# A two-layer gated cross-attention kernel: second attention's maxima through ScalarE and GpSimd, its first scores inside the first expert stage, its second half of queries placed by TensorE

## The reference

```python
x = x + tanh(g_xattn[0]) * attention0(layernorm(x), ctx)  # 16 heads of 64, causal mask
x = x + tanh(g_ffn[0])   * experts0(layernorm(x))         # 8 experts + 4 identity ones, top 2
x = x + tanh(g_xattn[1]) * attention1(layernorm(x), ctx)  # 16 heads of 8, no mask, biases
x = x + tanh(g_ffn[1])   * experts1(layernorm(x))         # 8 routed (top 2) + 2 shared experts
# attention1, per sequence and head:
attn = softmax(q @ k.T / sqrt(8)); out = (attn @ v) @ Wo.T + bo
```

## Time and profile before

| | |
|---|---|
| median of 3 runs | 275.26 us (273.01, 275.26, 275.41) |
| the profiled execution | 273.14 us, span 271.1 us from the first to the last instruction |
| busy: PE, DVE, ACT, POOL | 247.6, 190.0, 110.5, 69.6 us |
| first attention | to about 123 us |
| first expert stage | 123 to 184.4 us |
| second attention | 184.4 to about 231 us |
| second expert stage | to 267 us, then the store |
| mean granted TensorE clock | 0.996 of 2.4 GHz |

### The profile page before, as it was taken

How to read it: one execution, slowest core, us unless ns; L and a number is a source line. 1 busy time by engine, 2 the same in 40 slices (tenths; PEclk the granted TensorE clock), 3 DMA queues, 4 the chain that set the end, 5 groups by cost and what they waited for, 6 DMA issues and landing times.

```text
span 271.1 us, 7236 instructions
## 1 busy us (share of the span) xinstructions
PE 247.6 (91%) x2956; PEld 210.0 (77%) x2956; DVE 190.0 (70%) x478; ACT 110.5 (41%) x187; POOL 69.6 (26%) x83
## 2 busy tenths in 40 slices
PE   8879989899999999989999998998798988879992
PEld 3558878788998888769999997997576877757881
DVE  1537798967365989896256586438788998879753
ACT  2565545544441554323134453430636454221220
POOL 2355393445433533340010031001122001111000
PEclk9999999999999999999999999999999999999998
DMA  6519600030000000598499100340052000000011
GB/s 200 188 45 321 175 1 4 2 157 4 0 2 2 1 2 7 87 147 308 189 169 171 49 0 0 118 116 1 2 174 63 2 2 5 0 0 4 8 30 41
DMA packets 14705, 18.98 MB, mean 70 GB/s; under 512 B 2384, under 2 KB 11472, under 8 KB 14544
## 3 DMA queue, kind: packets, MB, share of 16 engines
q1 hardware_dynamic: 14528, 18.26, 25.6%
q10 hardware_dynamic: 144, 0.26, 0.5%
HBM read 13.80 MB, written 4.72 MB: 68 GB/s over the span
## 4 chain that ended last, share of the span: by engine, by line
PE 66%; DVE 16%; issue 5%; DMA 4%; ACT 4%; POOL 2%; SPq 1%; DVEq 0%
PE OC L1130 9%; PE MB L1090 5%; PE MB L980 5%; PE SP L1051 5%; PE OC L1073 5%; PE TP L1060 4%; PE MB L982 4%; PE MB L981 4%; PE TP L1243 3%; PE MB L1202 2%; PE MB L1206 2%; PE OC L1079 2%; DMA w_raw<-in_w 2%; PE SP L982 2%; PE SP L980 2%
## 5 line engine op out<-in xcount | busy, mean ns | idle before, releaser
L398 POOL TENSOR_TENSOR S_sb<-S_sb,nmax 128x512 f32<-128x512 f32 x32 | 33.2, 1039 | 38.9 <-DVE nmax L701 38.9
L798 DVE SCALAR_TENSOR_TENSOR x_sb<-OC,gate,x_sb 128x128 f32<-128x128 f32 x64 | 18.0, 345 | 26.8 <-PE OC L1130 26.8
L1130 PEld LDWEIGHTS OC<-f_w,hid 128*128 128x128 f32 x256 | 30.9, 192 | 1.4
L692 DVE TENSOR_TENSOR S_sb<-SP,maskb 128x512 f32<-128x512 f32 x32 | 21.9, 686 | 13.5 <-PE SP L1051 13.3
L1130 PE MATMUL OC<-f_w,hid 128*128 128x128 f32 x256 | 31.0, 275 | 0.0
L701 DVE TENSOR_REDUCE nmax<-S_sb 128x4 f32<-128x512 f32 x32 | 22.0, 686 | 1.1
L507 ACT ACTIVATE PT<-TP 128x512 f32<-128x512 f32 x32 | 19.0, 593 | 7.8 <-PE TP L1060 7.7
L1060 PE MATMUL TP<-id_sb,S_sb 128*128 128x128 f32 x128 | 19.6, 275 | 2.4 <-POOL S_sb L398 2.4
L368 POOL TENSOR_SCALAR var_eps<-mv 128x4 f32<-128x4 f32 x8 | 2.0, 245 | 70.9 <-DVE mv L646 70.9
L1073 PE MATMUL OC<-PT,arena_f 128*32 128x128 f32 x512 | 17.6, 275 | 2.3 <-issue 1.7
L1060 PEld LDWEIGHTS TP<-id_sb,S_sb 128*128 128x128 f32 x128 | 14.9, 141 | 5.6 <-POOL S_sb L398 3.9
(11 more groups left out here) (187 smaller groups left out, 582.5 us busy)
## 6 DMA issues: line engine op xcount, KB each, us to landing
arena_f<-in_zeros SPq DMA_DIRECT2D x1, 2048.0 KB, 14.5
w_raw<-in_w SPq DMA_DIRECT2D x4, 384.0 KB, 4.0
k_dram<-f_r SPq DMA_DIRECT2D x3, 512.0 KB, 13.9
arena_r<-k_dram SPq DMA_DIRECT2D x4, 384.0 KB
arena_r<-q_dram SPq DMA_DIRECT2D x16, 96.0 KB
ew_raw<-in_f0w SPq DMA_DIRECT2D x1, 1024.0 KB, 6.0
f_w<-in_f0w SPq DMA_DIRECT2D x1, 1024.0 KB, 9.8
row_dram<-f_r SPq DMA_DIRECT2D x2, 512.0 KB, 3.1
```

The costliest lines, as they stand in the source:

```text
L398: g.tensor_tensor(S_sb[:, b], S_sb[:, b], nmax[:, b].unsqueeze(2).to_broadcast([P, H4, P]), ALU.add).then_inc(shifted, 1)
L692: v.tensor_tensor(S_sb[:, b].rearrange("p (r a) k -> p r a k", r=2), SP[:, :, 2 * P * b:2 * P * (b + 1)].rearrange("p r (a k) -> p r a k", ...
L1130: ins = mm(OC[:, n % 2, batch(t)], hid[:, n % 2, c, batch(t)], f0_w2[:, e, c, :], start=(c == 0), stop=(c == 1))
```

## The change

It touches the second attention on all engines, the order of the first expert stage's second half, and the second expert stage's first steps.

- `shift1(b)` moves from VectorE to GpSimd. ScalarE first copies the transposed maxima to SBUF (`maxima1` on ScalarE, into `NMT`).
- The row sums of `outputs1` stand in 4 columns instead of being repeated over 128 (weights `row_of` in place of `col_sel_sb`). ScalarE copies values and sums to SBUF (`copy_outputs`), VectorE transposes the sums, takes the reciprocal of 16 numbers a partition and transposes back with a repeat; GpSimd multiplies (VectorE for the last sequence).
- Scores of sequence 0 and the first half of those of sequence 1 are computed inside the first expert stage (n = 13 to 15), in the ring banks (`SPARE`), with their maxima on VectorE at n = 12 and 13.
- Routing of the first expert stage's second half is one step sooner; `queries1(0)` is at n = 10 instead of 11.
- Keys and queries are placed by one DMA of all 128 partitions instead of four of 24 partitions; the DMAs that placed the rows of ones are gone. For the second half of the tokens there is no DMA at all: TensorE spreads the rows with 0/1 weights (`spread_queries`, 4 times 2 matmuls) and ScalarE copies them to `q1s` (`place_queries`).
- From sequence 3 on, `values_of(b - 2)` stands ahead of `maxima1(b)`, and `sums_of(b - 2)` behind the scores.
- The first half's output projection is one call; ScalarE scales it and GpSimd adds it to `x_sb` (`scale_output`, `residual1` on GpSimd).
- `keep_clock` runs: 24, 16, 16, 6 and 10 matmuls before, one of 12 now.
- VectorE in the last stage: `route_best(1, 0)` ahead of `normalise1(7)`, `route_gates(1, 0)` ahead of the loop; the second half's routing one step later.

```diff
+SPARE = [("s", 0, 0), ("s", 0, 1), ("t", 0, 0)]
+AREAS = [("s", 1, 0), ("s", 1, 1), ("t", 0, 1)]
@@ SyncE
-                for j in range(4):
-                    sp.dma_start(dst[32 * j:32 * j + 24, :, tok].bitcast(F32),
-                                 dram.rearrange("(j i) r t -> j r i t", j=4)[j]).then_inc(moved, 16)
+            def place_heads(dst, dram, moved):
+                sp.dma_start(dst.bitcast(F32), dram.rearrange("i p t -> p i t")).then_inc(moved, 16)
...
+            for w in range(2):
+                tok = slice(2 * P * w, 2 * P * (w + 1))
+                place_heads(q1s[:, :, tok], q_dram[:, :, tok], q_moved[w])
@@ GpSimd
+            def shift1(b):
+                pool.wait_ge(max_out, b + 1)
+                wait_queries(pool, b)
+                g.tensor_tensor(q1s[:, :, batch(b)], q1s[:, :, batch(b)].bitcast(F32),
+                                NMT[:].unsqueeze(1).to_broadcast([P, 4, P]), ALU.add).then_inc(shifted1, 1)
+            def residual1():
+                pool.wait_ge(scaled, 1)
+                g.tensor_tensor(x_sb[:, seqs(0), :], x_sb[:, seqs(0), :], xn[:, seqs(0), :], ALU.add).then_inc(res, 1)
+            def normalise1(b):
+                pool.wait_ge(o_sum1, 3 * (b + 1))
+                g.tensor_tensor(oT1[:, batch(b)], o_sb[:, b % 2, 0:P], R1[:, b % 2], ALU.mult).then_inc(o_done1, 1)
...
+            for b in range(2, B):
+                shift1(b)
+                if b == B - 2:
+                    residual1()
+                    continue
+                if b == B - 1:
+                    rstd_of(3, 0)
+                    normalise1(b - 3)
+                normalise1(b - 2)
                 for hook in hooks.get(b, ()):
                     hook()
@@ ScalarE
+            def maxima1(b):
+                name = ("m", b)
+                wait_full(act, name)
+                if b:
+                    act.wait_ge(shifted1, b)
+                sc.activation(NMT[:], ring(name)[:, 0:P], ACT.Copy).then_inc(max_out, 1)
...
+            for i in range(4):
+                place_queries(i)
+            hooks = {2: [lambda: split_f1(0), lambda: split_f1(1)], 3: [lambda: split_f1(2), lambda: split_f1(3)]}
+            for b in range(2, B):
                 for hook in hooks.get(b, ()):
                     hook()
+                if b > 2:
+                    copy_outputs(b - 2)
+                if b == B - 2:
+                    scale_output()
                 exp1(b, 0)
+                if b + 1 < B:
+                    maxima1(b + 1)
                 exp1(b, 1)
+            copy_outputs(B - 2)
             xnT_hi_copy(3, 0)
+            copy_outputs(B - 1)
@@ VectorE
             def normalise1(b):
...
+                dve.wait_ge(o_copied, b + 1)
+                v.transpose(sumT[:], o_sb[:, b % 2, P:2 * P].rearrange("p (c r) -> p c r", r=32)).then_inc(o_sum1, 1)
+                dve.wait_ge(o_sum1, 3 * b + 1)
+                v.reciprocal(rsum1[:], sumT[:, :, 0:4]).then_inc(o_sum1, 1)
...
+            xnT_lo_copy(3, 0)
             normalise1(B - 2)
-            xnT_lo_copy(3, 0)
+            route_best(1, 0)
             normalise1(B - 1)
-            route_best(1, 0)
...
+            route_gates(1, 0)
+            hooks = {0: [residual1, lambda: gates_lo(0), lambda: stats_after(3, 1)], 1: [lambda: normed(3, 1)],
```

More of the change, by code:

```diff
@@ L413, in _ @@
             pool.wait_ge(consts, 4)
-            for b in range(2):
+            for b in range(4):
                 const(row_of[:, b, b:b + 1], 1.0)
@@ new lines, in _ @@
+            xnT_lo_copy(2, 1)
+            max1(2, 0)
+            queries1(1)
+            max1(2, 1)
+            for b in range(2, B):
+                if b == B - 1:
+                    normalise1(b - 3)
+                    normed(3, 0)
+                    normalise1(b - 2)
+                    break
+                max1(b + 1, 0)
+                max1(b + 1, 1)
+                if b == B - 2:
+                    stats_after(3, 0)
+                else:
+                    normalise1(b - 2)
@@ L991, in fill_wait @@
                 name = ("w", b)
-                done(name, keep_clock(take(name)[:, 0:256], 16 if b < 2 else 6))
+                done(name, keep_clock(take(name)[:, 0:256], 12))
             def xn_transposes(n, h):
@@ L1189, in maxima1, with values_of @@
                 bank = take(name)
-                if b == 0:
-                    keep_clock(bank[:, 256:512], 24)
                 pe.wait_ge(maxed1, 2 * (b + 1))
                 done(name, nc.tensor.transpose(bank[:, 0:P], NM[:], id_sb[:]))
-            def outputs1(b):
+            def values_of(b):
                 bank = take(("o", b))
@@ L1205, in outputs1, with output1 @@
                         rows = slice(32 * j, 32 * (j + 1))
-                        ins = mm(bank[rows, P:2 * P], col_sel_sb[:, i, rows], PT1[b % 3][:, j, i, :],
+                        ins = mm(ring(name)[rows, P:2 * P], row_of[:, i, :], PT1[b % 3][:, j, i, :],
                                  start=(i == 0), stop=(i == 3))
-                done(("o", b), ins)
-            def output1(h, w):
-                name = ("y1", h, w)
+                done(name, ins)
+            def outputs1(b):
+                values_of(b)
+                sums_of(b)
+            def output1(h):
+                name = ("y1", h)
                 bank = take(name)
-                pe.wait_ge(o_done1, HB * h + 2 * w + 2)
-                for b in range(2):
-                    ins = mm(bank[:, batch(b)], oT1[:, batch(HB * h + 2 * w + b)], wo1_sb[:], start=True, stop=True)
+                pe.wait_ge(o_done1, HB * (h + 1))
+                for b in range(HB):
+                    ins = mm(bank[:, batch(b)], oT1[:, batch(HB * h + b)], wo1_sb[:], start=True, stop=True)
                 done(name, ins)
@@ L1358, in _ @@
                 if n == 2:
+                    xn_transposes(3, 1)
+                if n == 3:
                     logits(1, 1)
```

392 lines of the change are left out of this document (215 added, 177 removed).

## The result

| | median of 20 runs | lowest | profiled execution (span, mean granted clock) |
|---|---|---|---|
| before | 274.08 us | 272.15 | 273.14 us (271.1, 0.996) |
| changed | 276.16 us | 273.19 | 273.26 us (271.4, 0.985) |

The account below looks back on a forecast made before the run. TensorE and VectorE were taken to bound the attention's period together. 2.3 us gained less 0.7 lost made 1.6, so 273.14 became 271.5 us profiled, 273.7 from the median; forecast 272.5, range 267.5 to 277.

Parts of the forecast that it names:

- Step 1: First expert stage: 1.1 us gained from a wait, 1.0 us new wait at scores1(0, 0), last experts end at 186.5 us.
- Step 2: Opening of the second attention: transposed scores of sequence 3 start at 205.9 us, 2.0 us gained.
- Step 3: Steady sequences of the second attention: period 3.55 instead of 4.25 us, three exceptions, logits at 229.2, 2.3 us gained so far.
- Step 4: Last stage, logits to last expert group: 35.3 instead of 34.6 us, TensorE standing 2.8 us; 0.7 us lost.
- rival 3: TensorE's clock falls in the last stage's 2.8 us wait: 2.5 us lost, net 0.9 slower, 274.0 us; chance 0.12.
- My sum without a clock: Whole kernel: 2.3 us gained less 0.7 lost, 1.6 us gained, the profiled 273.14 becoming 271.5 us.
- rival 1: Queries land in time (1.0), and late shift 4 (1.9) or output1(0) wait (1.1) is absent: 4.5 us gained, 268.6; chance 0.28.
- Rival 2: GpSimd's shift decides every attention sequence: gain gone at 1.55 us a shift, 2.7 us lost at 2.0; chance 0.15.
- port rule: Last stage, GpSimd's product of sequence 6 beside the router: one engine held an estimated 0.4 us, making the gain 1.2 us.

Follow-up runs that it names:

- both_filled: Changed kernel with early exponential table and warm matmuls in the attention's opening, ahead of output1(1) and ahead of the second expert1: ratio to the kernel before 0.9952.
- exp_table: Changed kernel with one 128x1 exponential behind maxima1(0), so that its table is loaded early: ratio to the kernel before 1.0117.
- shift_vector: both_filled with the shifts of sequences 2 to 7 back on VectorE, reading ScalarE's copy of the maxima: ratio to the kernel before 0.9994.
- tail_fill: Changed kernel with 20 warm matmuls ahead of the wait of output1(1) and 16 ahead of the second expert1: ratio to the kernel before 0.9964.
- after_nofill: Changed kernel with its last warm matmuls cut from 12 to 1: ratio to the kernel before 1.0045, or 1.0147 by the medians of all runs.
- order_turn2: Changed kernel with VectorE's last-stage order rewritten, early exponential table, 26 warm matmuls in fill_wait(0), 5 each ahead of turned1(1,0) and turned1(2,0): ratio to before 0.9894.
- all_filled: tail_fill and exp_table together, with 26 warm matmuls in fill_wait(0) and 6 ahead of each turned1(b,0) from sequence 1 on: ratio to the kernel before 0.9999.
- opening_filled: Changed kernel with early exponential table, 26 warm matmuls in fill_wait(0), 5 each ahead of turned1(1,0) and turned1(2,0): ratio to the kernel before 1.0107.
- order_fill: Changed kernel with VectorE's last-stage order rewritten, early exponential table and 26 warm matmuls in fill_wait(0): ratio to the kernel before 0.9894.
- before_nofill: Kernel before without its warm matmuls of the second attention and last stage (two runs left out, three cut to one each): ratio to the kernel before 0.9998.
- stats_first: Changed kernel with VectorE's statistics of sequences 4 to 7 ahead of gates_lo(0): ratio to the kernel before 0.9933, or 1.0008 by the medians of all runs.

## Why the prediction was wrong

The step that failed is the last one of the sum, in two terms. It put nothing for TensorE's clock, which I had as a rival at 0.12 and at one place: the changed kernel was below full clock in all its 20 runs (0.942 to 0.985), and lost 0.2 us for each 0.001. And it put the last stage at 0.7 us lost: 1.9 were lost at full clock and 3.6 in the profiled run. At full clock 1.0 us of my 1.6 was there (both_filled); the clock took it and more.

**Step 1, the first expert stage: right, its wait too long.** The 1.19 us wait is gone (163.67, no idle). No wait of 1.0 us came at `scores1(0, 0)`: it ran at 176.19 behind `hidden0(14)`. The low part was done at 168.2 (168.7) and the placement issued 3.6 us later, the lower of the two values I had (3.6 and 5.3), and landed 4.0 us from its issue: taking the middle made the wait. Last experts end at 185.5, 1.0 us sooner than forecast.

**Step 2, the opening: right to 0.6 us, in part by luck.** Transposed 3 at 205.34 (forecast 205.9), though 19.9 us behind the last experts rather than 19.35: the microsecond won in step 1 hides half a one lost here. Of my chain one link was missing: the exponential's table, 1.28 us, is loaded only when its first input is there, at 186.24. exp_table shows that it cost next to nothing.

**Step 3, the steady sequences: right.** L417 takes 1.273 us (1.28). Sequence 4 waits 1.13 us for its shift behind the splits, period 4.83 (5.45); sequence 5 3.98 (3.55); `output1(0)` waits 0.94 (1.1); logits at 228.83 (229.2). What VectorE was relieved of by the shift did not matter at full clock, though: shift_vector.

**Step 4, the last stage: this failed.** "0.7 us lost" was 3.6. TensorE's wait of 2.8 us was 2.73, but I had second experts at 12.75 us and they came at 13.35; I counted the statistics ahead of the product, and not that TensorE would stand 2.27 us. At full clock the stage is 36.5 us (tail_fill), 1.2 over my 35.3; the clock adds 1.65. Of the 1.2, 0.35 is a slip of mine: second experts 0.35 later and 0.7 at n = 6 make 35.65, not 35.3. Another 0.55 is the second experts, and 0.3 lies in the steps up to n = 5; n = 6 cost 0.8, as put.

**The clock** was rival 3, with a price of 2.5 us, one place and a chance of 0.12. Its sign came, a clock under 1.0 between 225 and 250 us; that a fallen clock turns the gain into a loss was right, and the chance far too low. The 4 us of matmuls in its price had no row; a dip of 3.4 us costs this stage 1.6. I put it behind the 2.8 us wait only. It fell behind the shorter wait after it (in the profiled run), and in the attention, where I had looked for none because TensorE has no wait over 1.3 us there.

Most of the medians' loss will lie in the attention: the profiled run, with its dip in the last stage, is at 0.985 and 273.26 us; the median run, 2.9 us slower, is at 0.968. That its dips lie in the attention is not shown, for no trace of it was kept, but likely: in the traces of after_nofill and exp_table, at 0.962 and 0.959, 14 and 17 us of dips lie there and 7 and 3 in the last stage. What I had in hand and didn't weigh: the change takes out four of five runs of warm matmuls, shortens the other and makes TensorE the bound, so a stretch at 1.2 GHz that would have cost nothing before can cost now.

My sum without a clock, 271.5 us, stands against 271.6 of the profiled run without its 1.65, 271.05 us of tail_fill's one run at 1.000 and 271.8 of both_filled. That it comes so near is in part luck: the 1.2 us of order that I missed in the last stage are balanced by logits 0.4 us sooner than put and a store 0.6 us shorter, which I had not counted. Of rival 1 one term came, the queries' 1.0 us, of which half was lost again in the opening; the waits of 1.13 and 0.94 us stayed. Rival 2 didn't come: GpSimd's shift held 1.27 us in all eight.

On the port rule of the Trainium skill ("SBUF — State Buffer", "SBUF: two separate sides"): the product of sequence 6 ended at 230.16, before the router's first instruction with two SBUF inputs at 230.37, so it was not tested where I had put it. Elsewhere it was: `normed(3, 0)`, with two SBUF inputs, began 0.06 us behind a GpSimd product of 0.46 us and took 1.33 us; `normed(3, 1)`, beside none, 1.14. The trace agrees in direction, with 0.2 us in place of the 0.4 that the product still ran. The other traces with this product repeat it: 1.33 or 1.34 us beside it in each, and 1.13 or 1.14 beside none in every trace. So some contention is shown, but not the full block that the section states:
```profile
224.65 0.46 POOL L426 TENSOR_TENSOR oT<-o_sb,R 128x128 f32<-128x128 f32 x1
224.71 1.33 DVE L732 SCALAR_TENSOR_TENSOR xn<-x_sb,mv,rstd 128x128 f32<-128x128 f32 x4 [0.67 <-POOL rstd L382]
...
242.09 1.14 DVE L732 SCALAR_TENSOR_TENSOR xn<-x_sb,mv,rstd 128x128 f32<-128x128 f32 x4
```

**Still open:** why the clock falls in one run and holds in the next, of the same kernel with the same waits. That the waits which the change no longer fills bring it down is not shown for the attention: both_filled's fell where order_turn2's held, with the same waits to 0.16 us. Full-clock runs (0.99 and above) were more frequent with more warm matmuls, 9 of 12 in all_filled and 7 of 12 in both_filled against none of 20 in the changed kernel, but one of 6 in opening_filled and none of 6 in order_fill; I found no set that holds the clock always without standing in the way. And the mean clock is not the whole of the spread in the kernel before: at 0.985 to 0.987 it took anything from 275.1 to 280.7 us, and half the clock for that share of the span takes only 3.2 us from TensorE.

## What to carry to other kernels

When a change takes load off another engine and leaves TensorE the bound, look at its clock anew: warm matmuls that bought nothing before (before_nofill) may be needed, and a stretch at half clock that was nearly free (0.8 us of 17) now costs up to half its length (1.6 of 3.4 us in the last stage, 2.3 of 10 and 5.9 of 17 in the attention). The better cure for a wait is to shorten it: one engine's idle time in front of a wait (VectorE's 2.29 us here) is the place for work that stands behind it, and a chain that the next matmul needs belongs ahead of a longer one that it doesn't. Both together gave 2.6 us of order and 1.65 of clock with no instruction added. Judge such a kernel by many runs with their clocks, since its one profiled execution may be its best, and compare two kernels at the same clock.

## What the runs showed of the hardware

- 17 us of the second attention at 1.2 GHz cost the kernel before nothing measurable in the time (before_nofill, 0.9998) and 0.8 us in the trace; 17 us cost both_filled 5.9.
- The clock was at 0.50 for 17 us in which TensorE had no idle time (both_filled, busy 16.00 of 16.00 us), and it had fallen there with no wait over 0.41 us in the 17 us before.
- In the changed kernel the clock fell in the second of two waits of TensorE of 0.60 and 1.24 us with 8 small matmuls of 32 rows between them, and 0.8 us behind one of 2.27 us. In tail_fill it did not fall in the same two. It did not fall in the changed kernel's wait of 2.73 us (1.00 up to 242 us); in stats_first it did fall in the same wait, of 2.71 us, behind which the 8 matmuls took 2.05 us in place of 1.13. One and the same wait may or may not bring it down.
- The load of ScalarE's table (1.28 us) stood behind the wait of the exponential that needs it; a 128x1 exponential ahead moves it to 183.37, into idle time.
- The same shift of 128x512 takes 0.68 us on VectorE with the maxima from the bank (kernel before), 0.69 with them from SBUF (shift_vector), and 1.27 us on GpSimd.
- A layer norm's four VectorE instructions with two SBUF inputs took 1.33 us beside a GpSimd product of 0.46 us begun 0.06 us before, and 1.14 beside none.
